# Two-layer decoder on one core: the last pass of layer 1 interleaved with the shared-key heads before it

## The chip, the core and the metric

The kernel runs on one core of a Trainium2 chip. The metric is the device time of one execution in microseconds (us). The engines are TensorE (PE, its weight loads are PEld), VectorE (DVE), ScalarE (ACT), GpSimd (POOL) and SyncE (SP), which issues the DMAs here. Each engine works through its own instructions in program order and waits on semaphores for the others.

## What is computed

A decoder of two layers on an input of 8 tiles of 128 tokens by 256 features, all in float32. Each layer is self attention, cross attention and a feed-forward part, with a layer norm after each. The change touches the last two parts of layer 1, cut here to what matters:

```
# cross attention, 16 heads of 16; keys and values come from all 8 tiles (1024 rows)
q = fq_sym((x @ Wq + bq) * scale); k = fq_sym(k); v = fq_sym(v)
attn = fq_unsigned(softmax(q @ k.T))       # a row of 1024 for each token and head
x5 = layernorm(x4 + (attn @ v) @ Wp + bp)
# feed-forward, 768 hidden, weights rounded to fp8
gate = silu((x5 @ gate_w) * gate_scale); up = (x5 @ up_w) * up_scale
x6 = layernorm(x5 + ((gate * up) @ down_w) * down_scale)
```

## The kernel before

Layer 0 and the first two passes of layer 1 fill the first 1144 us; nothing of them is touched. What follows has two stages.

**The shared heads** (1144 to 1338 us). A loop over u = 0 to 127 (tile t = u // 16, head h = u % 16). For each u TensorE makes the scores, 128 by 1024 (L2263, two matmuls into the two PSUM banks of ps_s, ps_o or ps_t, by u % 3); VectorE takes their maximum (L1682) and one small step (L1684); ScalarE takes exp (L1060) and writes 16-bit integers with the row sum; SyncE issues a DMA transpose (L770); and five heads later (SUM_LAG) TensorE makes the sums with the values (L2274, eight small matmuls into ps_p). Scores u wait for exp u - 3 (three pairs of banks), and all of it is in program order on each engine. Once a tile's 16 sums are there, VectorE runs take_shared (L1670, L1671, L1675) at head 7 of the next tile.

**The third pass** (from 1338 us). For each tile n: out_turn (two transposes of the heads' output, L1807), a ScalarE copy (L844), out_project (two float32 matmuls with w_p2, recorded as four, L1791), in5 on VectorE (read with residual L1569, bias L1572, statistics L1573 to L1576), the power on GpSimd (L818), out5 (L1581), x5_turn (two transposes, L1807) and the split of x5 in three bf16 parts: first (ScalarE, L1068), rest (VectorE, L1711), second (ScalarE, L1070), last (VectorE, L1717). Four tiles are a half. For each half there are IB = 6 gate-and-up blocks, b = 0 to 5 and 6 to 11: twelve bf16 matmuls of 512 columns (L2304) into ps_s for even b and ps_o for odd b, tanh on ScalarE (gate, L1076), two steps on VectorE (gate_up_block, L1693 and L1696), and the split of the result in three parts (ScalarE L1081 and L1083, VectorE fuse_rest L1701 and fuse_last L1706). Then down for a tile (18 matmuls, L2314), in6 (L1569 or L1566, then L1572 to L1576), the power and out6 (L1581), and the store.

The order is written out by hand. Before block 0 the tiles 0 to 3 go through everything up to their last part, after all shared heads (PE waits for exp2 of all 128). The function beside(b) puts tile 4 + b beside block b for b = 0 to 3 and its x5 split one block later. In a block ScalarE runs gate, then both fuse parts, and only then the next block's gate. Block 6 waits for the parts of all 8 tiles (parts5). in6 and out6 of tiles 0 to 3 stand in blocks 8 to 11; the last four tiles' down sums come after block 11, two of them in ps_p and two in ps_t.

## Time and profile before

| | |
|---|---|
| Time, median of 3 runs | 1445.62 us (1440.58 to 1446.13) |
| Profiled execution | 1444.57 us, of which span 1442.8 us |
| PE busy over the span | 1288.0 us (89%) |
| DVE busy | 1072.3 us (74%) |
| ACT busy | 685.8 us (48%) |
| POOL busy | 102.2 us (7%) |

The page divides the span into 40 slices of 36 us. The stage of the shared heads is slices 32 to 37, where it shows DMA at 9 tenths and the granted clock at 5 tenths; the third pass is the last three slices:

```profile
PE   6979999998999999999999999988898589898676
DVE  6778578678578677757767755746888899999467
ACT  2336335435534633633543453523444388888232
PEclk9989999999999999999999999999999655555689
DMA  7321002001100100100200032002000199999000
```

Busy shares are means over stages. What a change in one stage is worth is read from that stage: who is late there, and what the others wait for.

### The profile page before, as it was taken

The page shows a single profiled execution, that of the slowest core. Times are in us where ns is not written, and L with a number is a line of the kernel's source. Part 1 is how long each engine was busy: PE and PEld are TensorE (multiplying, and loading weights), DVE is VectorE, ACT ScalarE, POOL GpSimd, SP SyncE. Part 2 cuts the span into 40 slices and gives each one's busy share as a digit, 9 for nine tenths or more (in the row PEclk, how much of TensorE's full clock was granted, in tenths as well). Part 3 has the DMA queues.
Part 4 walks back from the last instruction along what each step waited for, and adds up shares of the span by engine and source line. Part 5 has one row for each costly group of instructions (what it writes and reads, how often), then busy time and mean ns, then how long its engine had stood idle before and what let it go on. Part 6 is the DMA issues. An engine that isn't in the chain of part 4 may idle for free.

```text
span 1442.8 us, 24457 instructions
## 1 busy us (share of the span) xinstructions
PE 1288.0 (89%) x9108; PEld 854.2 (59%) x9113; DVE 1072.3 (74%) x2477; ACT 685.8 (48%) x1286; POOL 102.2 (7%) x95
## 2 busy tenths in 40 slices
PE   6979999998999999999999999988898589898676
PEld 3647667666766766766766676656777322222334
DVE  6778578678578677757767755746888899999467
ACT  2336335435534633633543453523444388888232
POOL 2210010020010011001002000000000000000001
PEclk9989999999999999999999999999999655555689
DMA  7321002001100100100200032002000199999000
GB/s 242 149 98 61 12 12 65 12 4 35 39 12 16 62 12 15 62 12 11 65 12 1 19 102 69 20 23 95 9 8 5 30 177 183 176 182 173 18 1 30
DMA packets 174789, 83.96 MB, mean 58 GB/s; under 512 B 137936, under 2 KB 170064, under 8 KB 174416
## 3 DMA queue, kind: packets, MB, share of 16 engines
q1 hardware_dynamic: 173520, 82.03, 23.6%
q8 instruction: 74, 1.21, 0.3%
q10 hardware_dynamic: 1152, 0.36, 0.1%
q14 instruction: 43, 0.35, 0.1%
HBM read 43.57 MB, written 5.24 MB: 34 GB/s over the span
## 4 chain that ended last, share of the span: by engine, by line
PE 59%; DVE 26%; ACT 5%; issue 5%; DMA 3%; POOL 1%; SPq 0%; DVEq 0%; POOLq 0%; ACTq 0%
PE ps_t L1807 12%; PE ps_p L1791 11%; PE ps_s L2040 7%; DVE w_moe L1682 7%; PE ps_o L1957 5%; PE ps_o L1947 4%; PE ps_o L1872 4%; PE ps_o L2040 3%; PE ps_p L1849 3%; DMA w_moe<-w_moe 3%; DVE probs L1203 2%; PE ps_s L1849 2%; PE ps_o L1876 2%; DVE row_max L1209 1%; DVE w_moe L1684 1%
## 5 line engine op out<-in xcount | busy, mean ns | idle before, releaser
L1807 PE MATMUL ps_t<-ident,probs 128*128 128x128 f32 x1072 | 170.4, 280 | 28.6 <-ACT probs L1022 8.0
L882 ACT ACTIVATE probs<-probs 128x512 f32<-128x512 f32 x184 | 115.6, 628 | 136.8 <-DVE probs L1203 136.8
L1807 PEld LDWEIGHTS ps_t<-ident,probs 128*128 128x128 f32 x1072 | 123.3, 142 | 78.1 <-issue 37.9
L844 ACT ACTIVATE probsT<-ps_t 128x512 f32<-128x512 f32 x232 | 136.5, 589 | 64.0 <-PE ps_t L1807 63.7
L2040 PE MATMUL ps_s<-w_moe,xbT 128*128 128x352 f32 x352 | 121.9, 471 | 0.0
L1791 PE MATMUL ps_p<-w_qkv,xinT 128*128 128x512 f32 (+1 forms) x240 | 105.1, 562 | 11.3 <-DMA xinT<-in_xT 7.4
L2274 PEld LDWEIGHTS ps_p<-vals,w_moe 128*128 128x128 f16 x1024 | 37.4, 106 | 120.1 <-DMA w_moe<-w_moe 100.6
L797 POOL TENSOR_TENSOR rms<-mean_sq,neg_half 128x8 f32<-128x8 f32 x40 | 67.1, 1679 | 269.2 <-DVE mean_sq L1237 269.2
L844 ACT ACTIVATE bigT<-ps_t 128x512 f32<-128x512 f32 (+1 forms) x128 | 69.0, 553 | 33.3 <-PE ps_t L1807 31.3
L2040 PEld LDWEIGHTS ps_s<-w_moe,xbT 128*128 128x128 f32 x352 | 64.1, 194 | 22.0 <-issue 1.4
L1872 PE MATMUL ps_o<-v_all,probsT 128*128 128x128 f32 x512 | 70.6, 282 | 6.6 <-DVE big L1267 6.2
L1957 PE MATMUL ps_o<-w_moe,bigT 128*128 128x256 f32 x288 | 70.9, 382 | 5.1 <-ACT bigT L844 5.1
L948 ACT ACTIVATE vals<-ps_s 128x176 f32<-128x176 f32 x88 | 27.9, 317 | 96.2 <-PE ps_s L2040 96.0
L1791 PEld LDWEIGHTS ps_p<-w_qkv,xinT 128*128 128x128 f32 x240 | 44.6, 193 | 48.2 <-issue 34.2
L1872 PEld LDWEIGHTS ps_o<-v_all,probsT 128*128 128x128 f32 x512 | 62.4, 193 | 12.7 <-DVE big L1267 11.2
L1957 PEld LDWEIGHTS ps_o<-w_moe,bigT 128*128 128x128 f32 x288 | 53.7, 190 | 20.7 <-ACT bigT L844 7.0
L1203 DVE TENSOR_TENSOR probs<-ps_p,row_max 128x512 f32<-128x512 f32 x88 | 60.2, 684 | 5.4 <-PE ps_s L1849 1.9
L2274 PE MATMUL ps_p<-vals,w_moe 128*128 128x16 f16 x1024 | 49.0, 177 | 15.3 <-DMA w_moe<-w_moe 14.7
L1194 DVE TENSOR_TENSOR probs<-ps_s,mask_in 128x512 f32<-128x512 f32 x60 | 40.9, 682 | 27.5 <-PE ps_s L1849 27.5
L789 POOL TENSOR_TENSOR rstd<-mean_var,neg_half 128x1 f32<-128x1 f32 x24 | 15.7, 655 | 625.5 <-DVE mean_var L1161 625.5
L1209 DVE TENSOR_REDUCE row_max<-ps_p 128x4 f32<-128x512 f32 x88 | 60.0, 682 | 0.0
L1807 PE MATMUL ps_t<-ident,big 128*128 128x128 f32 x400 | 58.9, 277 | 1.0 <-DVE big L1252 0.5
(317 smaller groups left out, 2679.9 us busy)
## 6 DMA issues: line engine op xcount, KB each, us to landing
w_out<-in_wT_out SPq DMA_DIRECT2D x8, 2048.0 KB, 8.5
w_moe<-in_wT_gu SPq DMA_DIRECT2D x1, 5632.0 KB, 17.6
w_moe<-in_wT_down SPq DMA_DIRECT2D x1, 2816.0 KB, 10.1
keys<-keys2T SPq DMA_DIRECT2D x8, 256.0 KB, 2.0
keys2T<-keys SPq DMA_DIRECT2D x1, 2048.0 KB, 10.2
w_moe<-w_moe SPq DMA_TRANSPOSE x128, 3.3
w_qkv<-in_wT_qkv SPq DMA_DIRECT2D x3, 512.0 KB, 4.9
w_qkv<-in_wT_qkv SPq DMA_DIRECT2D x1, 1536.0 KB, 8.2
```

The lines of the kernel that those rows point to most:

```text
L844: nc.scalar.activation(dst, src.bitcast(BF16) if dst.dtype == BF16 else src, ACT.Copy)\
L882: nc.scalar.activation(probs[:, at % 4, :], probs[:, at % 4, :], ACT.Exp).then_inc(L0.exped, 1)
L1203: nc.vector.tensor_tensor(q, q if is_masked(ahead) else scores_of(last), row_max[:, last % 4, :].unsqueeze(2).broadcast_to([P, GH, P]), AL ...
L1209: nc.vector.tensor_reduce(row_max[:, at % 4, :], p if is_masked(now) else scores_of(at), X, ALU.max)\
L1682: link1(nc.vector.tensor_reduce(max2[:, 0, h:h + 1], flat(shared_scores(u)[:]), X, ALU.max))
L1791: ins = nc.tensor.matmul(ps_p[:, n % 2, 0:width], xTi[:, k, :], w[:, k, col:col + width], start=(k == 0), stop=(k == last - 1))
L1807: ins = nc.tensor.transpose(dst[:, i * P:(i + 1) * P], src(i), ident_b[:] if bf else ident[:])
L1849: ins = nc.tensor.matmul(score_bank(at + j)[:, i * P:(i + 1) * P], q, k, start=kind == "x", stop=kind == "x" or i == GH - 1)
L1872: ins = nc.tensor.matmul(sliding_bank(t, g)[:, i * WIDE:(i + 1) * WIDE], turned_probs, wide(v0_wide, head0(g, i) // 4, HD0 + 1), start=Tru ...
L1957: ins = nc.tensor.matmul(ps_d[:, 0:D], hT_block(k), w_down[:, k, :], start=(k == 0), stop=(k == FB - 1))
L2040: ins = nc.tensor.matmul(ps_e[e % XB][:, 0:2 * F], xT[2][:, k, :], w_gu[:, k, 2 * F * e:2 * F * (e + 1)], start=(k == 0), stop=(k == KD - 1))
L2274: ins = nc.tensor.matmul(ps_p[:, av % 2, h * HD1:(h + 1) * HD1], n2T[:, v % TURNS, n * P:(n + 1) * P].bitcast(FP16), vals2[:, n, h * HD1:( ...
```

## The change

Third-pass work of tiles 0 to 3 moves into the loop of the shared heads. With n = t - 1: out_turn(n) on TensorE and its copy (oq_take) on ScalarE at head 9 of tile t, out_project(n) after the sums at head 12, in5(n) after head 13 and out5(n) after head 14. With n = t - 2: x5_turn at head 0 of tile t, then x5_first, x5_rest, x5_second and x5_last at heads 1, 3, 4 and 6. All these tiles use the bank of ps_p in which their own heads were summed (tile_bank); tiles 4 and 5 use ps_t. New semaphores (oq_turned, oq_taken, out2_done, x5_turned, second5) replace the shared counts, and the first sums of tiles 2 to 5 wait for rest5. The bias was added on VectorE before and is after; out_project has no third term.

In the last five turns of the loop (u = 128 to 132) TensorE also runs out_turn of 4, 5 and 6, out_project of 4 and 5, and the whole of block 0. Tiles 6 and 7 are finished between blocks 1 to 5. In the blocks the split of block b's result is one to two blocks late, so that ScalarE runs gate(b + 1) before fuse_second(b); down(d) comes in blocks 8 to 11, and the last four tiles' sums go to ps_t and ps_s. The two small steps on scales1 move ahead of the shared heads. No arithmetic is added or removed.

```diff
+OQ_TURN, OQ_TAKE, OUT2, IN5, OUT5 = 9, 9, 12, 13, 14
+X5_TURN, X5_FIRST, X5_REST, X5_SECOND, X5_LAST = 0, 1, 3, 4, 6
...
     keys += [("av", t) for t in range(TILES)]
-    keys += [("out2", t) for t in range(TILES)] + [("down", t) for t in range(HT + 2)]
+    keys += [("down", t) for t in range(HT)]
...
+        def last_sums(d):
+            return (ps_t if d < HT + 2 else block_banks(2 * IB - 2))[:, d % 2, 0:D]
...
+        def tile_bank(n):
+            if HT <= n < HT + 2:
+                return ps_t[:, n % 2, 0:D]
+            return ps_p[:, L1.p.at["av", n] % 2, 0:D]
...
+            def oq_take(n):
+                act.wait_ge(oq_turned, n + 1)
+                nc.scalar.activation(flat(lane_of(n).attT), tile_bank(n), ACT.Copy).then_inc(oq_taken, 1)
+            def x5_first(n):
+                act.wait_ge(x5_turned, n + 1)
+                nc.scalar.activation(x5p[:, 0, :, n * P:(n + 1) * P], turned_tile(n), ACT.Copy).then_inc(first5, 1)
+            def x5_second(n):
+                act.wait_ge(rest5, n + 1)
+                nc.scalar.activation(x5p[:, 1, :, n * P:(n + 1) * P], tmp_tile(n), ACT.Copy).then_inc(second5, 1)
...
-                nc.scalar.activation(x5p[:, 1, :, cols], tmp_tile(n), ACT.Copy).then_inc(L1.trans_taken, 1)
+                if 1 <= t <= HT and h == OQ_TAKE:
+                    oq_take(t - 1)
+                if 2 <= t <= HT + 1 and h == X5_FIRST:
+                    x5_first(t - 2)
+                if 2 <= t <= HT + 1 and h == X5_SECOND:
+                    x5_second(t - 2)
...
+            def fuse_first(b):
                 act.wait_ge(fused, b + 1)
                 nc.scalar.activation(fusep[b][:, 0, :], fuse[:, b % 2, :], ACT.Copy).then_inc(ffirst, 1)
+            def fuse_second(b):
                 act.wait_ge(frest, b + 1)
                 nc.scalar.activation(fusep[b][:, 1, :], tmpf[:, b % 2, :], ACT.Copy).then_inc(fsecond, 1)
...
-            for b in range(2 * IB):
-                n, x = beside(b)
-                if n is not None:
-                    turned("oq", n, lane_of(n).attT, D)
-                gate(b)
-                fuse_parts(b)
-                if x is not None:
-                    x5_parts(x)
+            oq_take(HT)
+            oq_take(HT + 1)
+            gate(0)
+            oq_take(HT + 2)
+            x5_first(HT)
+            gate(1)
+            fuse_first(0)
+            x5_first(HT + 1)
+            x5_second(HT)
+            oq_take(LAST)
+            gate(2)
+            fuse_first(1)
...
+            gate(5)
+            fuse_second(3)
+            x5_second(LAST)
+            fuse_first(5)
+            fuse_second(4)
+            gate(6)
+            for b in range(IB, 2 * IB):
+                if b + 1 < 2 * IB:
+                    gate(b + 1)
+                fuse_first(b)
+                fuse_second(b - 1)
+            fuse_second(2 * IB - 1)
...
-                if key == "down" and t >= HT + 2:
-                    dve.wait_ge(last_down, t - HT - 1)
-                    link1(nc.vector.tensor_tensor(res, ps_t[:, t % 2, 0:D], scale, op))
+                if key == "down" and t >= HT:
+                    dve.wait_ge(last_down, t - HT + 1)
+                    link1(nc.vector.tensor_tensor(res, last_sums(t), scale, op))
+                elif key == "out2":
+                    dve.wait_ge(out2_done, t + 1)
+                    link1(nc.vector.tensor_tensor(res, tile_bank(t), add, op))
...
+            dve.wait_ge(ld_w["scales1"], 16)
+            link1(nc.vector.tensor_scalar(scales1[:, 2, :], scales1[:, 0, :], 0.5, None, ALU.mult))
+            nc.vector.tensor_tensor(scales1[:, 3, :], scales1[:, 2, :], scales1[:, 1, :], ALU.mult)\
+                .then_inc(scaled_scales, 1)
+            dve.wait_ge(scaled_scales, 1)
...
+                if t >= 1 and h == TURN_LAG:
+                    take_shared(t - 1)
+                if 1 <= t <= HT and h == IN5:
+                    in5(t - 1)
+                if 1 <= t <= HT and h == OUT5:
+                    out5(t - 1)
+                if 2 <= t <= HT + 1 and h == X5_REST:
+                    x5_rest(t - 2)
+                if 2 <= t <= HT + 1 and h == X5_LAST:
+                    x5_last(t - 2)
...
-                d = b - IB - 2
+            in5(HT)
+            in5(HT + 1)
+            out5(HT)
+            out5(HT + 1)
+            gate_up_block(0)
+            take_shared(LAST)
+            x5_rest(HT)
+            gate_up_block(1)
+            in5(HT + 2)
+            fuse_rest(0)
+            x5_rest(HT + 1)
+            x5_last(HT)
+            gate_up_block(2)
+            out5(HT + 2)
+            in5(LAST)
+            fuse_last(0)
...
+            fuse_last(3)
+            fuse_rest(4)
+            for b in range(IB, 2 * IB):
+                d = b - IB - 3
                 gate_up_block(b)
-                if n is not None:
-                    in5(n)
+                fuse_last(b - 2)
+                if d >= 1:
+                    out6(d - 1)
+                fuse_rest(b - 1)
                 if d >= 0:
                     in6(d)
-                fuse_rest(b)
-                if n is not None:
-                    out5(n)
-                if d >= 0:
-                    out6(d)
-                fuse_last(b)
-                if x is not None:
-                    x5_rest(x)
-                    x5_last(x)
+            fuse_last(2 * IB - 2)
+            fuse_rest(2 * IB - 1)
+            out6(HT - 2)
+            in6(HT - 1)
+            fuse_last(2 * IB - 1)
+            out6(HT - 1)
             in6(HT)
-            in6(HT + 1)
-            out6(HT)
-            in6(HT + 2)
-            out6(HT + 1)
-            in6(HT + 3)
-            out6(HT + 2)
-            out6(HT + 3)
+            for d in range(HT + 1, TILES):
+                in6(d)
+                out6(d - 1)
+            out6(LAST)
         @block.tensor
...
+            def out_turn(n):
+                pe.wait_ge(heads_2, n + 1)
+                for k in range(KD):
+                    ins = nc.tensor.transpose(tile_bank(n)[:, k * P:(k + 1) * P], att2(n)[:, k * P:(k + 1) * P], ident[:])
+                ins.then_inc(oq_turned, 1)
...
+            def out_project(n):
+                pe.wait_ge(oq_taken, n + 1)
+                for k in range(KD):
...
+                ins.then_inc(out2_done, 1)
...
+                if b >= 2:
+                    pe.wait_ge(fused, b - 1)
+                else:
+                    pe.wait_ge(exp2, HEADS - 1 + b)
+                for i, w in ((0, w_gate1), (1, w_up1)):
...
                         pe.wait_ge(L1.proj_taken, av - 1)
+                        if 2 <= t <= HT + 1:
+                            pe.wait_ge(rest5, t - 1)
...
-                                                   x5p[:, part, k, half * HALF:(half + 1) * HALF],
-                                                   start=(k + part == 0), stop=(k == KD - 1 and part == 2))
-                ins.then_inc(gate_up1, 1)
+                t, h = u // H1, u % H1
+                if 1 <= t <= HT and h == OQ_TURN:
+                    out_turn(t - 1)
+                if 1 <= t <= HT and h == OUT2:
+                    out_project(t - 1)
+                if 2 <= t <= HT + 1 and h == X5_TURN:
+                    x5_turn(t - 2)
+                if u == HEADS:
+                    pe.wait_ge(exp2, HEADS - 2)
+                    out_turn(HT)
+                    out_turn(HT + 1)
+                if u == HEADS + 1:
+                    out_project(HT)
+                if u == HEADS + 2:
+                    out_turn(HT + 2)
+                    gate_and_up(0)
+                if u == HEADS + 3:
+                    out_project(HT + 1)
...
-            for b in range(2 * IB):
-                n, x = beside(b)
-                if n is not None:
-                    out_turn(n)
+            def last_blocks(d, blocks):
+                return down_blocks(d, last_sums(d), blocks)
+            x5_turn(HT)
+            out_project(HT + 2)
+            gate_and_up(1)
+            x5_turn(HT + 1)
+            out_turn(LAST)
+            gate_and_up(2)
+            out_project(LAST)
+            x5_turn(HT + 2)
+            gate_and_up(3)
+            gate_and_up(4)
+            x5_turn(LAST)
+            gate_and_up(5)
+            gate_and_up(IB)
+            gate_and_up(IB + 1)
+            for b in range(IB + 2, 2 * IB):
                 gate_and_up(b)
-                if n is not None:
-                    out_project(n)
-                if x is not None:
-                    x5_turn(x)
-                if IB < b <= IB + HT:
-                    down(b - IB - 1)
-            pe.wait_ge(L1.trans_taken, L1.t.done(0, ("x5", LAST)))
-            for d in (LAST - 1, LAST):
-                down_blocks(d, ps_t[:, d % 2, 0:D], range(IB - 1))
-            down(HT)
-            down(HT + 1)
-            for d in (LAST - 1, LAST):
-                down_blocks(d, ps_t[:, d % 2, 0:D], [IB - 1]).then_inc(last_down, 1)
+                down(b - IB - 2)
+            last_blocks(HT, range(IB - 1))
+            last_blocks(HT + 1, range(IB - 1))
+            pe.wait_ge(fused, 2 * IB - 1)
+            last_blocks(HT + 2, range(IB - 1))
+            last_blocks(LAST, range(IB - 1))
+            for d in range(HT, TILES):
+                last_blocks(d, [IB - 1]).then_inc(last_down, 1)
 _OUT = (TILES, P, D)
```

## Rows read from the trace of the kernel before

**Rows 1.** Stretches view, shared heads: PE, PEld, DVE, ACT, POOL busy, clock, DMA share, GB/s.
```profile
1200.00:1220.00 20.00, 17.85 (x132) 5.60 (x132) 19.09 (x31) 17.29 (x27) 0.00 (x0) 0.50 1.00 178
```

**Rows 2.** Waits view, shared heads, 1144 to 1338 us: total us, times, longest.
```profile
DVE w_moe L1682 <- PE ps_t L2263: 2.8, 5, 0.9
```

**Rows 3.** Timeline (start, length, engine, line, names), two undisturbed shared heads.
```profile
1209.28 1.21 DVE L1682 TENSOR_REDUCE w_moe<-ps_t 128x1 f32<-128x1024 f32 x1
...
1209.37 1.03 PE L2263 MATMUL ps_s<-keys2T,w_moe 48*128 48x512 bf16 x2
...
1210.66 1.21 DVE L1682 TENSOR_REDUCE w_moe<-ps_s 128x1 f32<-128x1024 f32 x1
```

**Rows 4.** Timeline, TensorE behind, catching up after a late transpose.
```profile
1159.80 1.03 PE L2263 MATMUL ps_t<-keys2T,w_moe 48*128 48x512 bf16 x2
...
1160.87 1.22 DVE L1682 TENSOR_REDUCE w_moe<-ps_t 128x1 f32<-128x1024 f32 x1 [0.91 <-PE ps_t L2263]
...
1161.08 1.03 PE L2263 MATMUL ps_s<-keys2T,w_moe 48*128 48x512 bf16 x2
```

**Rows 5.** Timeline, the echo of one take_shared.
```profile
1206.61 1.03 PE L2263 MATMUL ps_o<-keys2T,w_moe 48*128 48x512 bf16 x2 [1.11 <-ACT w_moe L1060]
```

**Rows 6.** Timeline, last shared head and first steps of the third pass.
```profile
1333.34 0.21 DVE L1684 TENSOR_SCALAR w_moe<-w_moe 128x1 f32<-128x1 f32 x1
...
1333.59 1.20 ACT L1060 ACTIVATE w_moe<-ps_o,w_moe 128x1024 int16<-128x1024 f32 x1
...
1338.67 1.09 PE L1807 MATMUL ps_t<-ident,w_moe 128*128 128x128 f32 x4
...
1340.79 2.08 PE L1791 MATMUL ps_p<-w_qkv,attT 128*128 128x256 f32 x4 [1.01 <-ACT attT L844]
...
1342.65 0.64 PE L1807 MATMUL ps_t<-ident,w_moe 128*128 128x128 f32 x2
```

**Rows 7.** Timeline, block 0: its first weight load and its tanh.
```profile
1358.80 0.13 PEld L2304 LDWEIGHTS ps_s<-w_out,w_x 128*128 128x128 bf16 x2 [1.39 <-DVE w_out L1717]
...
1363.71 0.69 ACT L1076 ACTIVATE squares<-ps_s,w_moe 128x512 f32<-128x512 f32 x1 [5.15 <-PE ps_s L2304]
```

**Rows 8.** Timeline, VectorE in one gate-and-up block of the first half.
```profile
1376.57 0.69 DVE L1693 SCALAR_TENSOR_TENSOR ropes<-squares,ps_s 128x512 f32<-128x512 f32 x1 [0.42 <-ACT squares L1076]
...
1377.96 0.42 DVE L1569 TENSOR_TENSOR xa<-ps_p,w_moe 128x256 f32<-128x256 f32 x1
...
1379.62 0.68 DVE L1701 TENSOR_TENSOR probs<-probs,keys2T 128x512 f32<-128x512 f32 x1
...
1380.75 0.41 DVE L1581 TENSOR_SCALAR w_moe<-xa,w_moe 128x256 f32<-128x256 f32 x1 [0.44 <-POOL w_moe L818]
...
1381.08 0.69 DVE L1706 TENSOR_TENSOR keys2T<-probs,keys2T 128x512 bf16<-128x512 f32 x1
...
1381.68 0.42 DVE L1711 TENSOR_TENSOR bigT<-ps_t,w_out 128x256 f32<-128x256 f32 x1
```

**Rows 9.** Groups by line and form, ScalarE, 1335 to 1443 us: busy, mean ns.
```profile
L1070 ACT ACTIVATE w_out<-bigT 128x256 bf16<-128x256 f32 x8 | 3.3, 416 | 9.5 <-DVE bigT L1711 9.5
```

**Rows 10.** Timeline, TensorE after four idle times of the third pass.
```profile
1369.15 1.13 PE L1791 MATMUL ps_p<-w_qkv,kdup 128*128 128x256 f32 x4 [1.81 <-ACT kdup L844]
...
1376.01 1.38 PE L1791 MATMUL ps_p<-w_qkv,attT 128*128 128x256 f32 x4 [2.70 <-ACT attT L844]
...
1395.56 2.74 PE L2304 MATMUL ps_s<-w_out,w_x 128*128 128x512 bf16 x6 [4.46 <-DVE w_out L1717]
...
1425.55 0.50 PE L2314 MATMUL ps_t<-w_qkv 128*128 128x256 bf16 x3 [2.59 <-DVE w_qkv L1706]
```

**Rows 11.** Timeline, one block period of TensorE in the second half.
```profile
1407.80 1.80 PE L2314 MATMUL ps_p<-w_qkv,keys2T 128*128 128x256 bf16 x15
...
1412.35 1.80 PE L2314 MATMUL ps_p<-w_qkv,keys2T 128*128 128x256 bf16 x15
```

**Rows 12.** Timeline, VectorE begins the norm of tile 4.
```profile
1431.33 0.42 DVE L1569 TENSOR_TENSOR bigT<-ps_p,w_qkv 128x256 f32<-128x256 f32 x1 [0.67 <-PE ps_p L2314]
```

More of the change, by code:

```diff
@@ L1688, in _, with x5_rest, x5_last @@
-            take_shared(LAST)
+            def x5_rest(n):
+                dve.wait_ge(first5, n + 1)
+                nc.vector.tensor_tensor(tmp_tile(n), turned_tile(n), x5p[:, 0, :, n * P:(n + 1) * P], ALU.subtract)\
+                    .then_inc(rest5, 1)
+            def x5_last(n):
+                cols = slice(n * P, (n + 1) * P)
+                dve.wait_ge(second5, n + 1)
+                nc.vector.tensor_tensor(x5p[:, 2, :, cols], tmp_tile(n), x5p[:, 1, :, cols], ALU.subtract)\
+                    .then_inc(parts5, 1)
@@ new lines, in in5, with out5 @@
+            def in5(n):
+                norm_in(N5, n, "out2", x4s[:, n], more=b_p2)
+            def out5(n):
+                norm_out(N5, n, x4s[:, n])
+            dve.wait_ge(ld_w["scales1"], 16)
[3 more added lines that the diff above has]
+            dve.wait_ge(scaled_scales, 1)
+            for u in range(TILES * H1):
+                t, h = u // H1, u % H1
+                q2s, max2 = q2ss[:, t], lane_of(t).max2
+                dve.wait_ge(s2, u + 1)
+                link1(nc.vector.tensor_reduce(max2[:, 0, h:h + 1], flat(shared_scores(u)[:]), X, ALU.max))
+                nc.vector.tensor_scalar(max2[:, 1, h:h + 1], max2[:, 0, h:h + 1], q2s[:, 2, h:h + 1], LN255,
+                                        ALU.mult, ALU.add).then_inc(max2_ready, 1)
+                if t >= 1 and h == TURN_LAG:
[8 more added lines that the diff above has]
+                    x5_last(t - 2)
@@ L1707, in fuse_last @@
                     .then_inc(fparts, 1)
-            def x5_rest(n):
-                dve.wait_ge(first5, n + 1)
-                nc.vector.tensor_tensor(tmp_tile(n), turned_tile(n), x5p[:, 0, :, n * P:(n + 1) * P], ALU.subtract)\
-                    .then_inc(rest5, 1)
-            def x5_last(n):
-                cols = slice(n * P, (n + 1) * P)
-                dve.wait_ge(L1.trans_taken, L1.t.done(0, ("x5", n)))
-                nc.vector.tensor_tensor(x5p[:, 2, :, cols], tmp_tile(n), x5p[:, 1, :, cols], ALU.subtract)\
-                    .then_inc(parts5, 1)
-            def in5(n):
-                norm_in(N5, n, "out2", x4s[:, n], more=b_p2)
-            def out5(n):
-                norm_out(N5, n, x4s[:, n])
             def in6(d):
@@ new lines, in _ @@
+            gate_up_block(2)
+            out5(HT + 2)
+            in5(LAST)
+            fuse_last(0)
+            fuse_rest(1)
+            x5_last(HT + 1)
+            gate_up_block(3)
+            out5(LAST)
+            x5_rest(HT + 2)
+            fuse_last(1)
+            fuse_rest(2)
+            gate_up_block(4)
+            x5_last(HT + 2)
+            fuse_last(2)
+            fuse_rest(3)
+            x5_rest(LAST)
+            gate_up_block(5)
+            x5_last(LAST)
+            fuse_last(3)
```

118 lines of the change are left out of this document (36 added, 82 removed).

## The prediction

> **What bounds it now.** The stretches view comes first, by stage. In the shared heads VectorE is busy 19.09 of 20 us, TensorE 17.85, ScalarE 17.29, the DMA engines all the time, and TensorE's granted clock is 0.50, its lower level of 1.2 GHz [rows 1]. Three resources look full, so the timeline must tell which one leads. One head takes 1210.66 - 1209.28 = 1.38 us, from one maximum on VectorE to the next [rows 3]. TensorE, when it is behind, makes a head in 1161.08 - 1159.80 = 1.28 us [rows 4]; it has 0.10 us to spare per head. VectorE begins a maximum 1.29 us after its scores began [rows 3], and as little as 1.07 us after when it is waiting for them [rows 4]: TensorE's lead is 0.22 us and can't grow, because scores u wait for exp u - 3. VectorE waits for TensorE only 2.8 us in five of its waits [rows 2] (about 3.6 us with two more of 0.4). So VectorE sets the pace here, the rest is close behind, and whatever is put on VectorE counts in full.
>
> The third pass is another matter. VectorE ends its last small step of the heads at 1333.34 + 0.21 = 1333.55 us [rows 6], block 6 starts on TensorE at 1395.56 [rows 10], in6 of tile 4 starts at 1431.33 [rows 12], the span ends at 1442.8. That is 62.0 us of opening and first half, 35.8 us of second half, and a tail of 11.5. In the first half a block takes VectorE from 1376.57 on through two block steps, in5, fuse_rest, out5, fuse_last and the x5 split [rows 8], with waits on ScalarE in between, because gate, first and second parts of one block follow each other. TensorE sits idle for 1.81, 2.70 and 4.46 us in this half [rows 10]. It is a stage of chains and waits; work that leaves it, and chains that overlap, shorten it.
>
> **What the change adds to the heads.** For each of tiles 0 to 3:
>
> VectorE: in5 1.67 us (1379.62 - 1377.96), out5 0.33 to 0.4 (1381.08 - 1380.75), two split steps of about 0.45 (0.42 busy) [rows 8]. That is 2.9 us, and VectorE is the pacemaker: 4 x 2.9 = 11.6 us. The two scale steps moved ahead of the loop add about 0.35.
>
> TensorE: out_turn is half of 1.09, 0.55 us; out_project is 1342.65 - 1340.79 = 1.86 us, or 1.72 without its first load [rows 6]; x5_turn 0.55. Where they stand decides their price. When VectorE stops for take_shared, TensorE gets an idle time of the same 1.1 us ahead of the scores four heads on [rows 5]. out_turn at head 9 falls in front of this echo of take_shared (head 7), and x5_turn at head 0 falls into the echo of in5 (head 13), which is 1.67 us long: I cost both at nothing, under that cover; without it they cost 0.55 - 0.22 = 0.33 each. out_project at head 12 has no echo over it. It delays the scores of head 13 by 1.72 to 1.86, less the lead of 0.22: VectorE waits 1.5 to 1.64, I take 1.57, four times = 6.3 us. in5 stands behind that wait and in turn holds TensorE, so the two add up.
>
> ScalarE: three copies of about 0.4 [rows 9]. Its exp and row-sum read end just before the next is due; a copy delays one exp by about 0.3, which TensorE's lead of 0.22 and the echoes take up. Nothing, between 0 and 4 x 0.3.
>
> GpSimd's power has a whole head (1.38) between in5 and out5. The wait on rest5 (x5_rest at head 3, sums asked for at turn 5) is over two heads early. The DMA queue is passed by nothing new; the longer stage gives its transposes air, and some of VectorE's 3.6 us of waits should fall into the new echoes: -0.7.
>
> Heads: 11.6 + 0.35 + 6.3 - 0.7 = **+17.6 us**.
>
> **What it takes from the third pass.** I follow it in the times of the run before, as if the heads still ended at 1333.55. Out_turn of 4 and 5: PE to 1334.8. out_project(4) waits for the last exp (1333.59 + 1.3 [rows 6]) and the copy, 1335.3 to 1337.1. Sums, out_turn(6), then block 0 at 1338.2. At the lower clock it takes 4.9 to 5.1 (before: from 1358.8 to the tanh at 1363.71 [rows 7]), so to 1343.2. Only behind it stands out_project(5), to 1344.7: VectorE, with in5(4), in5(5), out5(4), out5(5) in this order ahead of gate_up_block(0), idles from 1339.0 to 1344.75. It ends in5(5) at 1346.4 and out5(5), after the power, at 1347.75. From here to the last part of tile 7 it has 2 in5 (3.3), 2 out5 (0.7), take_shared(7) (1.1), 8 split steps less a half (3.4), 6 pairs of block steps of 1377.96 - 1376.57 = 1.39 (8.3), and 7 fuse steps of 1381.68 - 1381.08 = 0.60 (4.2) [rows 8]: 21.0 us, plus 1.8 of waits for the tanh of blocks 1, 3 and 5. Tile 7's parts are there at 1370.5. So block 6 starts 37.0 us after the heads and not 62.0: **-25.0 us**. Half of it is VectorE work that went into the heads, the rest waits.
>
> Second half, from block 6's start. It begins after a TensorE idle time of 3.8 us (block 5 ends at 1366.7), so at the lower clock as before (5.1 us). Then TensorE has a gate-and-up and a down in each of four blocks at 1412.35 - 1407.80 = 4.55 us [rows 11]; fused 11 comes 26.6 us after block 6's start. VectorE still has fuse_last 9 to 11, fuse_rest 10 and 11, in6 of 2 and 3, two out6: 7.0 us. TensorE's 48 matmuls of the last tiles begin to flow when fuse_last(10) is done (30.4) and take 5.2; in6(4) starts at about 36.0 against 35.8 before. **+0.2**. The tail (four in6, four out6, the store) keeps its 11.5.
>
> The clock. After idle times of 1.81 and 2.59 us TensorE still ran at the upper level (2.4 GHz): out_project in 1.13 us, three down matmuls in 0.50. After 2.70 and 4.46 it ran at the lower: 1.38 with slow blocks behind it, and six block matmuls in 2.74 [rows 10]. The new order has two idle times right at this edge: about 2.7 us ahead of x5_turn(6) (it waits for out5(6), which stands behind gate_up_block(2)), where the loss is 2.4 (block 3 in 5.1, not 2.7), and about 2.8 us inside the last sums, where it is about 2. I count one of the two: **+2.4**, between 0 and 4.4.
>
> Sum: 17.6 - 25.0 + 0.2 + 2.4 = -4.8. The profiled execution took 1444.57 us (span 1442.8, 1.8 around it), 1.05 below the median of the three runs; 1444.57 - 4.8 = **1439.8 us**, which I round to 1440.0.
>
> **A rule of the skill against a row.** The heads keep TensorE busy 17.85 of 20 us, and the granted clock stays at 0.50 throughout [rows 1]. The Trainium skill (TensorE: Matmul & The Clock Gate, Part 1) says that the lower clock is the default and that sustained activity releases the throttle; by that rule the heads should run at 2.4 GHz, and the row says that they don't. The rule does open a rival, C below: that full-array float32 projections among the heads tip it.
>
> **Rivals.**
>
> A. Slower: no echo covers anything. The pairs of banks couple three engines with a lead of 0.22 us, so it may be that each inserted step stops all of them for its full length. For it: TensorE, VectorE and ScalarE are each within 0.1 us of the 1.38 period, so a loss is never caught up. Against it: TensorE's 1.11 us wait four heads after take_shared [rows 5]. Its price: 4 x (0.55 + 0.55 on TensorE, 0.22 that I took off out_project, 1.2 on ScalarE) = 10.1, and 0.7 of waits that stay: 1440.0 + 10.8 = 1450.8, with both clock losses 1452.8. It is slower than before from the point at which 4.8 of the 10.8 us shows.
>
> B. The clock holds in both idle times, and block 0 finds the upper level, as TensorE comes to it without a pause: -2.4 and -2.4: 1435.2.
>
> C. The clock rises within the shared heads once out_project is among them. Each out_project then costs 1.03 in place of 1.8, heads -3.1, and B's gains with it: 1432.
>
> D. The overlap doesn't come about: VectorE's fixed order (two in5 and two out5 ahead of block 0's steps) has waits that I don't see, and the first half gives 20, not 25: 1445, no change. For it: VectorE is in program order and waits in turn on three engines; before, a block of the first half took 6.9 us where its VectorE work was some 6.
>
> **How the numbers follow.** Forecast 0.50, A 0.12, B 0.15, C 0.05, D 0.18. A measurement of this kernel can tell about 0.5%, 7.2 us, from no change: faster means below 1437.4, slower above 1451.8. The forecast's own range is 1436 to 1444, with one in seven of it below 1437.4. Faster: 0.07 + B 0.15 + C 0.05 and a rest of smaller sizes of the heads' cost, 0.06: 0.33. Slower: a half of A and the far end of D, 0.09. Same: 0.58. The range leaves out a part of A above and of C below: 1433 to 1450.
>
> **What would show it.** Right: the heads stage (first maximum to last small step) is 17 to 18 us longer at a granted clock of 0.50; VectorE waits for ps_p or the scores once per tile by about 1.5 us, right after L1791's matmuls, and no wait goes with the transposes; block 6 starts 37 us after the last head; in6 of tile 4 36 us after that; TensorE idle about 3.8 us ahead of block 6. Wrong: heads over 22 us longer (A), under 14 (C); a first half over 40 us (D); block 3 or the last down matmuls at the upper clock (B).

## The result and the profile after

The changed kernel takes 1434.55 us, median of 6 runs (1432.68 to 1436.52), beside 1445.19 us of the kernel before (6 runs, 1440.58 to 1446.64). The ratio is 0.9934, 95% interval 0.9919 to 0.9950: 0.66% faster, by some 10.6 us, where I had forecast 5.6 us (1440.0 beside 1445.62) and so "no change" as the likeliest outcome. Its profiled execution took 1434.54 us, span 1432.7 us (before 1444.57 and 1442.8).

The page of the kernel after, its slices of 36 us. The six slices with the clock at 5 tenths are the heads (five such slices before); the third pass, three slices before, has shrunk to little more than two:

```profile
PE   6979999999999999999999999988999689888876
...
PEclk9989999999999999999999999999999755555598
DMA  7332002000100100100200013002000099899800
```

Stretches view of after (us, then PE, PEld, DVE, ACT, POOL busy, clock, DMA share, GB/s): 20 us within the heads, all the heads, from there to block 6's first matmul, and from there to in6 of tile 4.

```profile
1200.00:1220.00 20.00, 18.58 (x132) 6.58 (x133) 17.94 (x32) 16.14 (x29) 0.00 (x0) 0.50 0.98 170
1146.00:1350.20 204.20, 179.13 (x1277) 59.49 (x1278) 189.79 (x313) 166.44 (x266) 2.19 (x4) 0.50 0.93 162
1350.20:1386.30 36.10, 26.73 (x135) 13.77 (x133) 23.85 (x60) 14.28 (x30) 3.04 (x4) 0.86 0.11 22
1386.30:1421.50 35.20, 32.50 (x210) 20.76 (x211) 26.07 (x57) 12.11 (x21) 2.95 (x4) 0.95 0.05 16
```

The first line answers [rows 1]: in a stretch with one whole insertion TensorE is busier (18.58 for 17.85), VectorE less busy (17.94 for 19.09), because it now waits. The clock is still 0.50.

Waits view of after, VectorE in the heads (total us, times, longest), to be put beside [rows 2]:

```profile
DVE w_moe L1753 <- PE ps_t L2370: 5.3, 5, 1.5
DVE w_moe L1753 <- PE ps_o L2370: 2.0, 2, 1.5
DVE w_moe L1753 <- PE ps_s L2370: 1.5, 1, 1.5
```

That is 8.8 us where the kernel before had 3.6. Four of these waits, 1.50 us each, stand behind out_project. The others, 2.9 us here and all of the 3.6 before, come each 1.4 us after TensorE had waited for a late DMA transpose. Among the ten profiles with work in the heads this part varies from 1.9 to 2.9 us, whatever the edit, so up to 1 us between two totals of the heads means nothing.

The timeline of after shows the pieces of one tile (start, length, engine, line, names; L1753 maximum, L1616 in5's read, L1729 the first of the two split steps):

```profile
1191.37 0.42 DVE L1616 TENSOR_TENSOR xa<-ps_p,w_moe 128x256 f32<-128x256 f32 x1
...
1193.03 1.22 DVE L1753 TENSOR_REDUCE w_moe<-ps_s 128x1 f32<-128x1024 f32 x1
...
1201.63 0.41 DVE L1729 TENSOR_TENSOR bigT<-ps_p,w_out 128x256 f32<-128x256 f32 x1
1201.96 1.22 DVE L1753 TENSOR_REDUCE w_moe<-ps_s 128x1 f32<-128x1024 f32 x1
```

From start to start, in5 takes 1193.03 - 1191.37 = 1.66 us, a split step 1201.96 - 1201.63 = 0.33, and out5 between two maxima, read in the same way, 0.32. And the next tile's TensorE steps, still in the timeline of after (L2323 out_turn, L2329 out_project, L2370 scores):

```profile
1209.03 0.69 PE L2323 MATMUL ps_p<-ident,w_moe 128*128 128x128 f32 x2
1209.65 1.03 PE L2370 MATMUL ps_s<-keys2T,w_moe 48*128 48x512 bf16 x2
...
1211.74 1.03 PE L2370 MATMUL ps_o<-keys2T,w_moe 48*128 48x512 bf16 x2 [0.74 <-ACT w_moe L1084]
...
1214.33 2.05 PE L2329 MATMUL ps_p<-w_qkv,kdup 128*128 128x256 f32 x4
...
1216.31 1.03 PE L2370 MATMUL ps_s<-keys2T,w_moe 48*128 48x512 bf16 x2
...
1217.38 1.22 DVE L1753 TENSOR_REDUCE w_moe<-ps_s 128x1 f32<-128x1024 f32 x1 [1.50 <-PE ps_s L2370]
```

out_turn takes 0.62 us of TensorE, and VectorE doesn't wait behind it. An echo is the idle time that TensorE gets a few heads after VectorE has stopped for other work; of take_shared's echo, 1.11 us in [rows 5], 0.74 us are left at 1211.74. ScalarE's copy (0.37 us) stands between two exps, and no wait follows it. Behind out_project VectorE waits 1.50 us, and so in all four tiles.

The third pass of after, TensorE and the two long waits of VectorE (L2351 gate-and-up, L2336 x5_turn, L2415 down, L1613 in6's read of tile 4):

```profile
1350.03 0.21 DVE L1754 TENSOR_SCALAR w_moe<-w_moe 128x1 f32<-128x1 f32 x1
...
1354.27 0.36 PEld L2351 LDWEIGHTS ps_s<-w_out,w_x 128*128 128x128 bf16 x2
...
1354.49 3.88 PE L2351 MATMUL ps_s<-w_out,w_x 128*128 128x512 bf16 x12
...
1358.41 0.69 ACT L1098 ACTIVATE squares<-ps_s,w_moe 128x512 f32<-128x512 f32 x1 [6.29 <-PE ps_s L2351]
...
1359.63 0.42 DVE L1616 TENSOR_TENSOR kdup<-ps_t,w_moe 128x256 f32<-128x256 f32 x1 [3.79 <-PE ps_t L2329]
...
1372.57 0.44 PE L2336 MATMUL ps_p<-ident,w_moe 128*128 128x128 f32 x2 [3.02 <-DVE w_moe L1631]
1372.85 4.36 PE L2351 MATMUL ps_o<-w_out,w_x 128*128 128x512 bf16 x12
...
1377.96 0.69 DVE L1770 SCALAR_TENSOR_TENSOR ropes<-squares,ps_o 128x512 f32<-128x512 f32 x1 [2.25 <-ACT squares L1098]
...
1386.31 4.20 PE L2351 MATMUL ps_s<-w_out,w_x 128*128 128x512 bf16 x12 [3.47 <-DVE w_out L1735]
...
1415.69 0.50 PE L2415 MATMUL ps_t<-w_qkv 128*128 128x256 bf16 x3 [2.69 <-DVE w_qkv L1783]
...
1421.54 0.42 DVE L1613 TENSOR_TENSOR bigT<-ps_t,w_qkv 128x256 f32<-128x256 f32 x1 [1.79 <-PE ps_t L2415]
```

By stage, in the same cuts for both kernels:

| us | before | predicted | after |
|---|---|---|---|
| up to the first maximum | 1144.7 | +0.35 | 1145.8 |
| heads, first maximum to last small step | 188.9 | +17.25 | 204.5 |
| to block 6 | 62.0 | -22.6 (a clock loss of 2.4 in it) | 36.1 |
| block 6 to in6(4) | 35.8 | +0.2 | 35.2 |
| to the end of the span | 11.5 | 0 | 11.2 |

The first line moves by itself: the first maximum falls between 1140.4 and 1147.8 in the profiles of this study, in kernels that are the same up to there but for two small steps. A single profile's total is therefore good to some us only, and the stages are what is compared below. They come from one profile of each kernel, the times from four runs or more.

### The profile page after: what moved, and what is told of

The parts are those of the page before. It is cut to its first block, busy times and chain, and to the rows that moved or that the text cites. A ratio compares the mean times of both kernels' runs of the same rounds, so it can differ in the third digit from the quotient of the medians.

```text
span 1432.7 us, 24438 instructions
## 1 busy us (share of the span) xinstructions
PE 1290.0 (90%) x9113; PEld 854.0 (60%) x9113; DVE 1069.5 (75%) x2477; ACT 682.4 (48%) x1286; POOL 100.5 (7%) x95
## 4 chain that ended last, share of the span: by engine, by line
PE 64%; DVE 24%; issue 4%; ACT 4%; DMA 2%; POOL 1%; ACTq 0%; SPq 0%; DVEq 0%; POOLq 0%
PE ps_t L1877 12%; PE ps_p L1861 11%; PE ps_s L2110 8%; DVE w_moe L1753 6%; PE ps_o L2027 5%; PE ps_o L2017 4%; PE ps_o L1942 4%; PE ps_o L2110 3%; PE ps_p L1919 3%; DVE probs L1250 2%; PE ps_s L1919 2%; PE ps_o L1946 2%; DMA w_moe<-w_moe 2%; DVE row_max L1256 1%; DVE w_moe L1754 1%
## 5 line engine op out<-in xcount | busy, mean ns | idle before, releaser
L855 ACT ACTIVATE bigT<-ps_t 128x512 f32<-128x512 f32 (+1 forms) x128 | 68.9, 553 | 33.1 <-PE ps_t L1877 31.2
L2110 PEld LDWEIGHTS ps_s<-w_moe,xbT 128*128 128x128 f32 x352 | 64.8, 196 | 22.6 <-issue 2.2
L1942 PEld LDWEIGHTS ps_o<-v_all,probsT 128*128 128x128 f32 x512 | 62.4, 192 | 12.7 <-DVE big L1314 11.2
L2017 PE MATMUL ps_o<-w_out,bigT 128*128 128x256 f32 x224 | 59.3, 392 | 0.0
```

The costliest lines, as they stand in the source:

```text
L855: nc.scalar.activation(dst, src.bitcast(BF16) if dst.dtype == BF16 else src, ACT.Copy)\
L1942: ins = nc.tensor.matmul(sliding_bank(t, g)[:, i * WIDE:(i + 1) * WIDE], turned_probs, wide(v0_wide, head0(g, i) // 4, HD0 + 1), start=Tru ...
L2017: ins = nc.tensor.matmul(out0_bank(n), o0T[k // 4][:, k % 4, :], w_out0[:, k, :], start=(k == 0), stop=(k == 15))
L2110: ins = nc.tensor.matmul(ps_e[e % XB][:, 0:2 * F], xT[2][:, k, :], w_gu[:, k, 2 * F * e:2 * F * (e + 1)], start=(k == 0), stop=(k == KD - 1))
```

## The experiments

T is the account of the prediction: VectorE leads in the heads with TensorE 0.22 us ahead, an echo covers what is put in front of it, the rest counts in full. Under each kernel stand its time as a ratio to the kernel before, and the three stages of its profile (heads; to block 6; to in6(4)).

### The changed kernel again

> The changed kernel once more, as the measure for the others of this call: 1434.5 us, 10 to 11 below the kernel before. If theory T (below, in the next runs) is right, its shared heads take 204 to 205 us from the first maximum to the last small step, VectorE waits about 1.5 us once per tile behind out_project, and block 6 starts 36 us after the last head.

Measured: ratio 0.9932 (0.9918 to 0.9947); 204.5, 36.1, 36.5 us. Heads and first half repeat to 0.1 us. The second half is 1.3 us longer, and one line of this run's timeline says why: the last sums came back from their idle time slowly, 0.82 us for three matmuls where after had 0.50.

```profile
1416.18 0.82 PE L2415 MATMUL ps_t<-w_qkv 128*128 128x256 bf16 x3 [2.69 <-DVE w_qkv L1783]
```

### Tiles 0 to 3 behind the heads, the new order of blocks kept

The edit moves more than tiles 0 to 3. What TensorE did in the last five turns of the loop (out_turn of tiles 4 to 6, out_project of 4 and 5, block 0) comes behind tiles 0 to 3 too, and take_shared(7) comes ahead of all of it.

```diff
-                if 1 <= t <= HT and h == IN5:
-                    in5(t - 1)
...
+            take_shared(LAST)
+            in5(0)
+            in5(1)
+            out5(0)
+            out5(1)
+            x5_rest(0)
...
+            pe.wait_ge(exp2, HEADS)
+            out_turn(0)
+            out_turn(1)
+            out_project(0)
...
+            gate_and_up(0)
+            out_project(HT + 1)
```

> One part alone: the new order of blocks and of tiles 4 to 7 stays, but tiles 0 to 3 stand behind the shared heads again, in the order of the kernel before (their banks are now halves of ps_o and ps_s). Theory T: both parts pay. The heads lose their 16 us again (189 us), the opening costs its 25 us up to block 0 again, plus about 2.5 for the turns and the projection of tiles 4 to 6 ahead of block 0, and blocks 0 to 5 keep their new 32 us against 36.8: 1441.5 us, 3.5 under the kernel before, 7 over the change. Rival 1, the move among the heads carries the whole gain: 1445. Rival 2, the order of the blocks carries it: 1437 or less.

Measured: 0.9971 (0.9959 to 0.9983); 189.8, 55.6, 36.8 us. The heads are those of before again, to 0.9 us, and the waits behind late transposes account for that (4.8 us here, 3.6 before). The time falls in two parts: the new order of blocks alone brings 1445.2 - 1440.85 = 4.4 us (62.0 to 55.6, less 1.0 in the second half), and moving the tiles and the opening of the third pass into the heads another 1440.85 - 1435.6 = 5.2 us beside the repeat of after on the same chip: it costs 14.7 in the heads and saves 19.5 behind them. So neither part does it alone, and the move isn't a plain exchange of VectorE work: of the 19.5 us only 10.6 are work of VectorE. How the rest divides between the tiles and the work of the last five turns wasn't tried.

### The second half without its pipelining

```diff
             for b in range(IB, 2 * IB):
-                if b + 1 < 2 * IB:
-                    gate(b + 1)
+                gate(b)
                 fuse_first(b)
-                fuse_second(b - 1)
+                fuse_second(b)
...
-            for b in range(IB + 2, 2 * IB):
+            for b in range(IB + 1, 2 * IB):
                 gate_and_up(b)
-                down(b - IB - 2)
+                if b <= IB + HT:
+                    down(b - IB - 1)
```

> The change with its second half (blocks 6 to 11) undone: ScalarE runs gate, first and second part of one block before the next gate, VectorE both fuse steps in their own block, down one block earlier, as before. Theory T: TensorE sets this half (four gate-and-ups with four downs at 4.55 us) and VectorE the end of it, whichever way ScalarE is ordered; the traces give 35.8 us before and 35.2 after from block 6 to in6 of tile 4. So +0.5 us over the change, 1435. Rival: running one block deep is what pays there; then about +3 us, 1437.5, with VectorE's wait for ScalarE back at 0.7 us twice a block.

Measured: 0.9932 (0.9917 to 0.9946); 204.6, 36.1, 34.9 us. The order one block deep is worth nothing in the second half. The likely reason, read from the trace and not tried by itself, is that TensorE is busy there 32.50 of 35.20 us in after, so that an earlier tanh or split gives it nothing to start sooner. VectorE waits only 0.74 us for the last sums instead of 1.79.

### Block 3 ahead of x5_turn(6)

```diff
             out_project(LAST)
-            x5_turn(HT + 2)
             gate_and_up(3)
+            x5_turn(HT + 2)
             gate_and_up(4)
```

> The change with one swap on TensorE: block 3 ahead of x5_turn(6), which in the change waits 3.0 us for out5(6), after which block 3 ran at the lower clock (4.4 us). Theory T with the clock as I priced it: block 3 needs only fused 1, so it runs in that pause at the upper clock (2.75 us), the pause of 3 us is gone, its tanh comes 4 us earlier and VectorE starts gate_up_block(3) about 2.2 us earlier: block 6 starts 34 us after the last head, not 36, and the time is 1432.3. Rival, VectorE is the bound of the first half whatever TensorE does: no change, 1434.5.

Measured: 0.9923 (0.9907 to 0.9940); 203.75, 34.7, 35.2 us. Block 3 now starts without an idle time and takes 2.75 us and not 4.36. The first half gains only 1.4 us. In this run block 1 took 4.38 and not 2.75 us, at the lower level, behind 2.05 us of idle time that the others with this wait came out of at the upper one; and 1.2 to 1.4 us is also what two kernels without this swap gained where block 3 happened to run at the upper level (34.7 with half of out_project, 34.8 with the transposes in the echo). What the swap is worth beyond that is seen only in the kernel with all three improvements. The rows of blocks 1 and 3 here:

```profile
1357.44 0.44 PE L2336 MATMUL ps_t<-ident,w_moe 128*128 128x128 f32 x2 [2.05 <-DVE w_moe L1631]
...
1358.64 4.38 PE L2351 MATMUL ps_o<-w_out,w_x 128*128 128x512 bf16 x12
...
1366.75 2.75 PE L2351 MATMUL ps_o<-w_out,w_x 128*128 128x512 bf16 x12
```

### out_project(5) ahead of block 0

```diff
                 if u == HEADS + 1:
                     out_project(HT)
+                    out_project(HT + 1)
                 if u == HEADS + 2:
                     out_turn(HT + 2)
                     gate_and_up(0)
-                if u == HEADS + 3:
-                    out_project(HT + 1)
```

> The change with out_project(5) right behind out_project(4), ahead of out_turn(6) and block 0. VectorE, whose order asks for in5(5) before gate_up_block(0), waits 3.8 us for it behind block 0 in the change. Theory T: in5(5) can follow in5(4) at once; block 0 starts 1.9 us later, but gate_up_block(0) starts 1.5 us earlier, and as VectorE is the bound of the first half, block 6 is 1.5 us earlier, 34.5 us after the last head: 1434. Rival, TensorE's order is what counts there: block 0 later by 1.9 us makes it 1437.

Measured: 0.9932 (0.9910 to 0.9954); 204.2, 34.5, 36.75 us. The first half is 1.6 us shorter, as worked out. The profile's total shows nothing of it, since the last sums ran slowly here (VectorE waited 3.46 us for them, 1.79 in after), and the median of 1434.8 us can't be told from the 1434.55 of after.

### Half of out_project for tiles 0 to 3

This kernel leaves out half of that projection, so its result isn't the decoder's; it serves to price the step.

```diff
-                for k in range(KD):
+                kk = range(1 if n < HT else KD)
+                for k in kk:
```

> The change with the second of the two matmuls of out_project left out for tiles 0 to 3 (half of that projection isn't computed); tiles 4 to 7 are whole. It measures the price of out_project among the heads. Theory T: VectorE's wait behind it is its length less TensorE's lead of 0.22 us: 0.86 - 0.22 = 0.64 us where the change has 1.50, so the heads are 3.4 us shorter (204.4 to 201), time 1432. Rival 1: the wait is a fixed cost of stopping the three-bank ring: still about 1.5 us, 1435.5. Rival 2: the DMA transposes set the stage and the wait only moves: the four waits fall, but TensorE's waits for the transposes grow by as much, 1435.

Measured: 0.9906 (0.9881 to 0.9930); 200.65, 34.65, 36.7 us. The timeline:

```profile
1214.79 1.20 PE L2330 MATMUL ps_p<-w_qkv,kdup 128*128 128x256 f32 x2
...
1216.99 1.23 DVE L1753 TENSOR_REDUCE w_moe<-ps_s 128x1 f32<-128x1024 f32 x1 [0.65 <-PE ps_s L2371]
```

TensorE is 0.85 us shorter and the wait goes from 1.50 to 0.65 us, 0.85 as well. What out_project takes of TensorE beyond the lead is paid by VectorE one to one; the heads gain 3.85 us, 3.4 of them in these four waits. Both rivals fall: a fixed cost would have left 1.5 us, and if the DMA transposes set the pace the other waits would have grown, but they are 2.3 us and not 2.9.

### out_project moved into the echo of take_shared

```diff
-OQ_TURN, OQ_TAKE, OUT2, IN5, OUT5 = 9, 9, 12, 13, 14
+OQ_TURN, OQ_TAKE, OUT2, IN5, OUT5 = 9, 7, 10, 13, 14
```

> The change with OQ_TAKE = 7 and OUT2 = 10 in place of 9 and 12: ScalarE's copy falls into its own idle time behind take_shared, and out_project into what is left of TensorE's echo (0.74 us after out_turn in the trace). Theory T, work in an echo is free: VectorE's wait falls from 1.50 to 1.8 - 0.74 - 0.22 = 0.85 us a tile, heads 2.6 us shorter, time 1433. Rival: there are no echoes to fill, what hid out_turn was the lead: the wait stays at 1.5 or grows to 1.5 + 0.55, as both stand close together: 1435.5 to 1438.

Measured: 0.9915 (0.9885 to 0.9945); 202.4, 36.1, 35.2 us. The same instructions, two heads earlier, and the wait of the second and third tile is 0.78 and 0.79 us and not 1.50: the 0.74 us that were left of the echo take up that much of out_project. In the first tile it is 1.60 and in the fourth 1.24. There TensorE had waited 0.90 and 0.87 us for a DMA transpose just before VectorE stopped for take_shared, so it came to out_project late. The four waits together are 4.4 us and not 6.0; the other 0.5 us of the heads' gain is in the waits behind late transposes and no merit of the edit.

That a late transpose uses up the cover wasn't tried by itself, but the same shows elsewhere. The kernel with all three improvements has 1.24 and 0.86 us of lateness in its first and fourth tile and waits of 1.71 and 1.24 us there, 0.79 in the others. With out_turn alone in the echo, VectorE waits for nothing in the first tile behind 0.89 to 1.12 us of lateness (five profiles), and 0.16 and 0.19 us behind 1.26 and 1.29.

```profile
1174.03 0.38 PE L2384 MATMUL ps_p<-vals,w_moe 128*128 128x16 f16 x8 [0.90 <-DMA w_moe<-w_moe]
...
1181.68 1.22 DVE L1753 TENSOR_REDUCE w_moe<-ps_s 128x1 f32<-128x1024 f32 x1 [1.60 <-PE ps_s L2370]
...
1208.36 1.23 DVE L1753 TENSOR_REDUCE w_moe<-ps_o 128x1 f32<-128x1024 f32 x1 [0.78 <-PE ps_o L2370]
```

### Two transposes more, within the echo and outside

The first kernel issues out_turn's transposes twice where they stand, the second issues the same two again ahead of out_project; tiles 0 to 3 only.

```diff
-                for k in range(KD):
+                for k in list(range(KD)) * (2 if n < HT else 1):
                     ins = nc.tensor.transpose(tile_bank(n)[:, k * P:(k + 1) * P], att2(n)[:, k * P:(k + 1) * P], ident[:])
```

> The two transposes of out_turn are issued twice for tiles 0 to 3, at the same place (head 9), so TensorE has 0.62 us more there, four times; the result is unchanged. In the changed kernel TensorE still waits 0.74 us for exp two scores later (1211.74), the rest of take_shared's echo. Theory T (an echo covers what is put in front of it, up to its length): the 0.74 us shrink to about 0.1, VectorE waits for nothing new, heads 204.5 us as in the changed kernel, 1434.6. Rival A (each inserted step stops all three engines for its length less the lead of 0.22 us, or all of it): four times 0.4 to 0.62, heads 206.1 to 207.0, 1436.2 to 1437.1.

```diff
                 pe.wait_ge(oq_taken, n + 1)
+                for k in range(KD if n < HT else 0):
+                    nc.tensor.transpose(tile_bank(n)[:, k * P:(k + 1) * P], att2(n)[:, k * P:(k + 1) * P], ident[:])
```

> The same two extra transposes for tiles 0 to 3, but right ahead of out_project at head 12, where VectorE already waits 1.50 us for the scores behind out_project and no echo stands over it; the result is unchanged. Theory T: each adds its whole 0.62 us to that wait (2.1 us instead of 1.50), four times: heads 204.5 + 2.5 = 207.0 us, 1437.1. Rival A says the same here, so the pair of runs is what tells: T wants a difference of 2.5 us in the heads between two kernels with the same instructions, A wants none or at most 0.9.

Measured: within the echo 0.9913 (0.9897 to 0.9930); 203.7, 34.8, 36.7 us. Outside 0.9925 (0.9906 to 0.9943); 205.2, 35.85, 35.2 us. The first timeline is of the kernel with the four transposes in the echo:

```profile
1211.10 1.12 PE L2323 MATMUL ps_p<-ident,w_moe 128*128 128x128 f32 x4
1212.15 1.03 PE L2370 MATMUL ps_s<-keys2T,w_moe 48*128 48x512 bf16 x2
...
1213.81 1.03 PE L2370 MATMUL ps_o<-keys2T,w_moe 48*128 48x512 bf16 x2 [0.32 <-ACT w_moe L1084]
...
1219.45 1.22 DVE L1753 TENSOR_REDUCE w_moe<-ps_s 128x1 f32<-128x1024 f32 x1 [1.50 <-PE ps_s L2370]
```

and the second of the kernel with two of them ahead of out_project:

```profile
1213.98 0.67 PE L2329 MATMUL ps_p<-ident,w_moe 128*128 128x128 f32 x2
...
1214.44 1.91 PE L2331 MATMUL ps_p<-w_qkv,kdup 128*128 128x256 f32 x4
...
1216.29 1.03 PE L2372 MATMUL ps_s<-keys2T,w_moe 48*128 48x512 bf16 x2
...
1217.36 1.23 DVE L1753 TENSOR_REDUCE w_moe<-ps_s 128x1 f32<-128x1024 f32 x1 [1.82 <-PE ps_s L2372]
```

In the echo TensorE is 1.05 - 0.62 = 0.43 us later, the leftover wait falls from 0.74 to 0.32, and the heads are no longer than in after. This holds in three of the four tiles; in the first, TensorE had waited 1.18 us for a late transpose, and VectorE then waited 0.50 us behind the doubled out_turn:

```profile
1181.41 0.38 PE L2384 MATMUL ps_p<-vals,w_moe 128*128 128x16 f16 x8 [1.18 <-DMA w_moe<-w_moe]
...
1184.20 1.09 PE L2323 MATMUL ps_p<-ident,w_moe 128*128 128x128 f32 x4
...
1186.30 1.23 DVE L1753 TENSOR_REDUCE w_moe<-ps_t 128x1 f32<-128x1024 f32 x1 [0.50 <-PE ps_t L2370]
```

Outside the echo TensorE is 0.33 us later (2.31 from the first transpose to the scores, 1.98 without), and all of it lands in VectorE's wait, 1.50 to 1.82. Rival A, by which each insertion stops everybody, is out: it wanted the heads 1.6 to 2.5 us longer in the first kernel, and they are 0.7 shorter. T's size was wrong, though: I had taken 0.62 us for two transposes, but right behind others or ahead of a projection they add 0.43 and 0.33. So the heads of the two kernels differ by 1.5 us where I expected 2.5; 1.3 of it is in the four waits.

### The three improvements together

Block 3 first, out_project(5) first and out_project in the echo: the three diffs above in one kernel.

> The three moves together: block 3 ahead of x5_turn(6), out_project(5) ahead of block 0, out_project of tiles 0 to 3 at head 10. Theory T adds them, as they lie in different stretches: 2.1 (measured for the first), 1.5 and 2.6 off 1435.6: 1429.4, 1.1% under the kernel before. Rival: the first half has one bound and the first two do not add: 1431.

Measured: 1429.26 us (1427.01 to 1432.82), ratio 0.9899 (0.9872 to 0.9925); 203.2, 31.2, 35.2 us. It is 15 us faster than the kernel before and about 5 faster than the changed one. The total is the one expected, 1429.4, though its interval holds the rival's 1431 too, and its parts came otherwise. The first half falls by 36.1 - 31.2 = 4.9 us where 3.6 were expected. Of that 1.6 is out_project(5), as when tried alone, and the other 3.3 goes with block 3 first and with blocks 1 to 5 all at the upper clock in this profile. The heads gain 1.3 us where 2.6 were expected: the four waits fall by 1.5 us, as with the same edit alone (1.6), and the waits behind late transposes differ by the rest. That the total agrees so well is luck.

## Why the prediction was wrong in size

The mechanisms of the forecast held. Its sum, -4.8 us, was 5 us short of the profile's -10.0; the measured 1434.55 lies inside the range (1433 to 1450) and outside the forecast's own (1436 to 1444). The outcome that I called likeliest, no change, didn't come: by the bound of 0.5% the kernel is faster.

- **Heads: +17.25 predicted without the scale steps, +15.6 measured.** The structure was right in every part, but the sign that I had named, heads 17 to 18 us longer, didn't come. VectorE waits once per tile behind out_project, 1.50 us (predicted 1.57). in5 is 1.66 (1.67) and out5 0.32. The mis-sized term is the split: I charged about 0.45 us a step and it takes 0.33, eight times, 1.0 us. In [rows 8] the next instruction begins 0.33 us after out5's start (1380.75 to 1381.08), less than its recorded 0.41; I had read the start-to-start time there and not for the splits. The rest, by measured sizes: 4 x (1.66 + 0.32 + 0.33 + 0.33) = 10.6, and waits 8.8 - 3.6 = 5.2: 15.8 against 15.6. The -0.7 for waits that fall into the new echoes came out (3.6 to 2.9), but the scatter of these waits is as large, so that agreement is luck.
- **Echoes.** Both transposes cost nothing under them, as predicted, and the pair of kernels with doubled transposes shows for out_turn that it is the echo that pays; for x5_turn in the echo of in5 there is only the trace, in which no wait goes with it. The prediction left out what a late DMA transpose does to the cover. What I didn't ask is whether out_project could have one: two thirds of take_shared's echo went unused. Its use takes 1.5 to 1.6 us off the four waits.
- **To block 6: -25.0 + 2.4 = -22.6 predicted, -25.9 measured.** out5(5) ends 12.3 us after the heads, not 14.2. The failing step is "at the lower clock it takes 4.9 to 5.1": block 0 takes 1358.41 - 1354.27 = 4.1 us from its first load to its tanh, since the clock rises within it, and it begins 4.0 and not 4.65 us after the heads; out_project(5) behind it takes 1.2 and not 1.5. The clock's part is a part of rival B. From there to block 6 I had 21.0 us of VectorE work (measured 20.5) and 1.8 + 2.4 = 4.2 us of waits (measured 1.06 + 2.25 = 3.3). The 2.4 for one block at the lower clock was too much: behind the same idle time, the profiles with block 3 at the upper clock reach block 6 1.2 to 1.4 us sooner.
- **The second half: +0.2 predicted, -0.5 measured**, and the tail 0.3 shorter. Taking the pipelining away gives 34.9: what the new order does here is nothing that can be told from none, and the sign of so small a term wasn't known.
- **The clock.** I counted one of two idle times, and in the profile of after it is one: block 3 at 4.36 us, the last sums fast. The repeat lost both. That is a matter of the run, as the last section says; 1.4 us for block 3 and 1.3 to 1.5 for the last sums put up to 3 us of scatter under every total here.
- **The starting point.** The profile of after reached its first maximum 1.1 us later than before, 0.35 by the moved scale steps; no term for it was wrong.

In sum: heads 1.65, first half 3.3, second half and tail 1.1, less 0.7 at the start make the 5.3 us.

**Rivals.** A fell by the pair of doubled transposes and by the four waits, which together with the work of VectorE account for the heads. C fell by the granted clock of 0.50 in all the heads. D fell: the first half takes 36.1 us and not over 40. B came in part: block 0 ended at the upper clock, and of its two signs the last sums ran at the upper clock and block 3 didn't.

The Trainium skill (TensorE: Matmul & The Clock Gate, Part 1) says that the lower clock is the default and that activity releases it. The case's traces agree with it behind the heads, where block 0 begins at the lower clock and ends at the upper; they disagree within them, where TensorE is busy 179.13 of 204.20 us, by the stretch above, and stays at 0.50, and four float32 projections among the heads change nothing in that. No run here shows what about the heads' instructions keeps it so.

## What to carry to other kernels

In a ring of buffers with one engine in the lead, ask of each inserted step whose time it takes: on the leading engine it counts in full, on another it counts only beyond its lead, and nothing at all if it stands where that engine must wait anyway for an earlier stop of the leader, and hasn't lost that time to something else, here a late transpose. So pair insertions: put the other engines' extra work into the echo of the leader's extra work, and look whether a longer piece fits there too. And read the length of a short instruction from start to start of a queue that has no gaps: here the recorded lengths overlap, 0.41 for 0.33 us.

## What the runs showed of the clock

TensorE's clock after one and the same idle time isn't the same from run to run. Ahead of block 3 there are nine profiles with 3.02 or 3.03 us of idle time: in six (after, its repeat, the serial second half, out_project(5) first, out_project in the echo, the transposes outside) block 3 took 4.06 to 4.44 us, in three (the tiles behind, half of out_project, the transposes in the echo) it took 2.75 or the pace of that. Inside the last sums, 2.69 us of idle time was followed by matmuls at the lower level in five of ten profiles; in four of these the first three were still fast (0.50 us). Behind 2.05 us, or nearly that, ahead of block 1 it happened once in nine (the kernel with block 3 first), and there too the matmuls right behind were still fast. The 3.47 us ahead of block 6 ended at the lower level in all eleven. The stretches view from the turn ahead of block 3 on, first after, where the stretch ends with block 3, then the kernel with half of out_project, where it takes in most of block 4 too:

```profile
1372.60:1377.20 4.60, 4.60 (x15) 1.94 (x16) 2.97 (x9) 0.00 (x0) 0.93 (x1) 0.63 0.00 0
```

```profile
1370.80:1376.00 5.20, 5.20 (x25) 2.50 (x26) 4.38 (x12) 2.00 (x4) 0.93 (x1) 1.00 0.00 0
```

The granted clock is 0.63 in the one and 1.00 in the other, behind 3.02 and 3.03 us. Block 3 at the lower level takes 1.6 us longer (4.36 for 2.75). In a forecast for such a kernel, an idle time like those of 2.05, 2.69 and 3.02 us here, which ended at either level, should be carried as a chance, or taken out, as putting block 3 first did. Nothing here shows what decides it.
